# Graph attention layer on one core: preparation and edge stage in one block, no clearing of the sums, first markings inside the q loop, twelve blocks normalised on GpSimd

## The reference

```python
h = relu(layernorm(x))
q, k, v = h @ wq + bq, h @ wk + bk, h @ wv + bv
scores = sum(q[dst] * k[src], -1) / 16 + edge_weight * we + be
attn = softmax of scores over the edges of each dst
out = segment_sum(v[src] * attn, dst)
y = layernorm(h + out + h @ ws + bs) * g1 + b1
z = layernorm(y + gelu(y @ w_ff1 + b_ff1) @ w_ff2 + b_ff2) * g2 + b2
return x + z
```

## Time and profile before

| what | us |
|---|---|
| median of three runs (2398.57 to 2403.62) | 2402.55 |
| profiled execution, its own time | 2402.3 |
| its span, first to last instruction | 2400.5 |
| busy: PE / DVE / ACT / POOL | 2212.3 / 1757.4 / 1168.5 / 1653.7 |
| load of an activation table on ACT | 1.28 |
| a store of 512 KB of h, issue to landing, median | 6.7 |

### The profile page before, as it was taken

The page is one execution under the profiler, slowest core; times in us unless marked ns, Lnnn a source line. Parts: engine busy times, 40 slices in busy tenths (PEclk is TensorE's granted clock), DMA queues, the critical chain, the costliest instruction groups (busy, mean ns, idle before and its releaser), DMA issues. The chain is left out here.

```text
span 2400.5 us, 69609 instructions
## 1 busy us (share of the span) xinstructions
PE 2212.3 (92%) x14709; PEld 1867.1 (78%) x14710; DVE 1757.4 (73%) x7359; ACT 1168.5 (49%) x2903; POOL 1653.7 (69%) x1828
## 2 busy tenths in 40 slices
PE   6789889898999999999999999999999999989995
PEld 4678767776777777877887888888888888877884
DVE  7668667676777777777777777777778888774378
ACT  5545444444444444444444544555445555454454
POOL 4747777777777777777777777777777777402356
PEclk8989999999999999999999999999999999989997
DMA  8344444444444444444444444444444444350014
GB/s 266 103 116 139 137 138 136 137 138 137 139 137 137 136 137 138 138 138 139 136 138 137 137 138 136 138 135 137 137 140 136 139 140 137 89 159 0 0 53 135
DMA packets 148118, 311.09 MB, mean 130 GB/s; under 512 B 33550, under 2 KB 84609, under 8 KB 148088
## 3 DMA queue, kind: packets, MB, share of 16 engines
q0 software_dynamic: 75264, 205.62, 29.7%
q1 hardware_dynamic: 54702, 90.19, 11.7%
q10 hardware_dynamic: 18122, 14.96, 2.0%
HBM read 290.21 MB, written 20.43 MB: 129 GB/s over the span
## 5 line engine op out<-in xcount | busy, mean ns | idle before, releaser
L831 POOL DMA_INDIRECT work<-h_rows,idx x1536 | 1461.4, 951 | 483.2 <-issue 445.4
L919 PE MATMUL bank<-work 128*128 x3520 | 836.5, 380 | 0.0
L1010 DVE SCALAR_TENSOR_TENSOR work<-bank,work 128x257 bf16<-128x257 f32 x1764 | 646.7, 424 | 231.7 <-SPq L795 200.3
L856 PE MATMUL bank<-q,onehot 128*128 x5304 | 740.2, 274 | 70.2 <-DVE work L1010 52.7
L919 PEld LDWEIGHTS bank<-work 128*128 128x128 f32 x3520 | 634.6, 190 | 78.9
L856 PEld LDWEIGHTS bank<-q,onehot 128*128 128x128 bf16 x5304 | 510.2, 98 | 154.6 <-issue 92.6
L967 ACT COPY work<-bank 128x256 f32<-128x256 f32 x880 | 285.5, 377 | 397.5 <-PE bank L906 395.0
L963 ACT ACTIVATE work<-work 128x1 f32<-128x1 f32 x440 | 129.6, 295 | 624.5 <-DVE work L1076 624.5
L1076 DVE CUSTOM_DVE_ANT_0 work<-bank,work 128x512 f32<-128x512 f32 x440 | 329.8, 750 | 108.7 <-PE bank L862 77.1
L964 ACT ACTIVATE work<-work 128x512 f32<-128x512 f32 x440 | 311.6, 708 | 0.0
L906 PE MATMUL bank<-ident,work 128*128 128x128 f32 x1760 | 266.7, 274 | 29.0 <-ACT work L964 29.0
(11 more groups left out here) (192 smaller groups left out, 1601.7 us busy)
## 6 DMA issues: line engine op xcount, KB each, us to landing
dst_words<-dst_short SPq DMA_DIRECT2D x99, 512.0 KB
work<-h_rows,idx POOLq DMA_INDIRECT x1568
bias<-h_rows ACTq DMA_DIRECT2D x56, 128.0 KB
r_rows<-bias ACTq DMA_DIRECT2D x55, 128.0 KB
work<-r_rows SPq DMA_DIRECT2D x49, 128.0 KB, 2.1
acc<-in_x SPq DMA_DIRECT2D x4, 1536.0 KB, 15.7
h_rows<-acc SPq DMA_DIRECT2D x12, 512.0 KB, 6.7
work<-in_x SPq DMA_DIRECT2D x12, 512.0 KB, 3.9
```

The costliest lines, as they stand in the source:

```text
L831: pool.indirect_dma_start(rows[:, u, j, 0:D], None, h_rows, bass.IndirectOffsetOnAxis(idx[:, half, u * J + j:u * J + j + 1], 0)).then_inc( ...
L856: last = nc.tensor.matmul(banks[j][:, 0:D1], onehot[:, k, j, :], q3[:, bass.ds(b, 1), c, 0:D1], start=(c == 0), stop=(c == 2))
L919: last = nc.tensor.matmul(banks[6 + k][:, 0:D1], probs[:, j, :], rows[:, bass.ds(slot, 1), j, :], start=(j == 2), stop=(j == 1))
L1010: last = nc.vector.scalar_tensor_tensor(out=product[:, j, 0:D1], in0=banks[j][:, 0:D1], scalar=SCALE, in1=rows[:, bass.ds(slot, 1), j, :], ...
```

## The change

Preparation and edge stage become one block. The five memsets of `acc` (`clear`) go: a first sum is multiplied by a decay of 0 where a node has edges, and at the end nodes without edges are multiplied by 0 through `inv_sum`. The first two markings, the read of the maxima and what they need stand in DVE's iteration 40 of the q loop (`MARKED_AT`). POOL normalises blocks 28 to 35 and 44 to 47, before its cast of the list and not behind it. `layer_factors` loses a copy. Each engine takes over its part of the edge stage behind its last instruction of the preparation, with waits where the barrier stood. `product` lies before `outside` in SBUF now. The bodies of the edge stage's loops are moved, not changed.

```diff
-    BY_POOL = range(FULL - 8, FULL)
+    BY_POOL = [*range(28, 36), *range(FULL - 4, FULL)]
+    MARKED_AT = 40
...
+        def normalised(b):
+
+            if b in BY_POOL:
+                return h_done_by_pool, BY_POOL.index(b) + 1
+            return h_done, sum(1 for k in range(b + 1) if k not in BY_POOL)
...
-            dve.wait_ge(ln_link, 5 * turn + 5)
-            nc.vector.scalar_tensor_tensor(out=nmr[:, blocks], in0=mean[:, blocks], scalar=-1.0, in1=rstd[:, blocks], op0=ALU.mult, op1=ALU.mult).then_inc(ln_link, 1)
-            dve.wait_ge(ln_link, 5 * turn + 6)
-            nc.vector.tensor_copy(tmp[:, blocks], nmr[:, blocks]).then_inc(ln_done, 1)
+            dve.wait_ge(ln_link, 4 * turn + 5)
+            nc.vector.scalar_tensor_tensor(out=nmr[:, blocks], in0=mean[:, blocks], scalar=-1.0, in1=rstd[:, blocks], op0=ALU.mult, op1=ALU.mult).then_inc(ln_done, 1)
...
             @block.gpsimd
-                pool.wait_ge(list_in, 3 * 16)
-                g.tensor_copy(dst_s[0:EDGE_P, :], dst_a[0:EDGE_P, :]).then_inc(dst_cast, 1)
-
-                pool.wait_ge(ln_done, 4)
-                for n, half in enumerate((BY_POOL[0:4], BY_POOL[4:8])):
+                for n, half in enumerate((BY_POOL[0:4], BY_POOL[4:8], BY_POOL[8:12])):
+                    pool.wait_ge(ln_done, 4 if half[-1] >= QUARTERS[3][0] else 3)
...
+                pool.wait_ge(list_in, 3 * 16)
+                g.tensor_copy(dst_s[0:EDGE_P, :], dst_a[0:EDGE_P, :]).then_inc(dst_cast, 1)
...
-                def clear(k):
-                    first, end = k * XG, (k + 1) * XG if k < 4 else NB
-                    pool.wait_ge(h_out[k], 3 * 16 if k < 4 else 16)
-                    pool.wait_ge(hT_ready, min(end, B))
-                    pool.memset(acc[:, first:end, :], 0.0)
...
-                for k in range(5):
-                    clear(k)
+
+                pool.wait_ge(plan_done, 1)
+                n, m, rounds = counts(pool)
...
             @block.scalar
+                act.wait_ge(plan_done, 1)
+                nc.scalar.activation(decay[:, 1:2], eps[:, 0:1], ACT.Exp, scale=0.0).then_inc(sums_set, 1)
+                act.wait_ge(biases_split, 1)
+                act.wait_ge(h_out[0], 3 * 16)
+                act.dma_start(h_in, h_rows[0:P, :]).then_inc(h_back, 16)
+                act.sem_inc(r_stored, 16)
+                prepare(0, 0)
+                prepare(1, 1)
...
             @block.vector
+                nc.vector.memset(acc[:, 0:FULL, D:D1], 0.0)
...
+                def mark_first_steps():
+
+                    for k in range(4):
+                        dve.wait_ge(h_out[k], 3 * 16)
+                    dve.wait_ge(h_out[4], 16)
+                    dve.wait_ge(tab_copied, 6)
+                    dve.wait_ge(plan_done, 1)
+                    nc.vector.memset(banks[7][:, 0:D1], 0.0).then_inc(sums_set, 1)
+                    dve.load(regs[0:3], steps_tab[0:1, 0:3])
+                    ahead[:] = [dve.snap(v, min_val=0, max_val=TP * BLOCKS) for v in regs[0:3]]
+                    blocks[:] = [block_of(dve, v) for v in ahead]
+                    dve.sem_inc(added, 1)
+                    dve.sem_inc(max_kept, 1)
+                    dve.sem_inc(onehot_done, S)
+                    mark(place_of_mark(ahead[0]), 0)
+                    mark(place_of_mark(ahead[1]), 1)
+                    read_max(0, 0, blocks[0])
...
+                    if b == PLAN + 2:
+                        dve.wait_ge(biases_split, 1)
+                        nc.vector.memset(rows[:, :, :, D:D1], 1.0).then_inc(ones_set, 1)
+                    if b == MARKED_AT:
+                        mark_first_steps()
...
+                dve.wait_ge(lo_done, B)
+                edge_scores(ahead[0], 0, 0, 0)
+                dve.wait_ge(outside_done, 1)
+                mark(place_of_mark(ahead[2]), 0)
+                dve.wait_ge(sums_set, 2)
...
             @block.tensor
+                pe.wait_ge(plan_done, 1)
                 pe.load(regs[0:2], steps_tab[0:1, 0:2])
                 ahead = [block_of(pe, pe.snap(v, min_val=0, max_val=TP * BLOCKS)) for v in regs[0:2]]
                 pe.sem_inc(summed, S)
                 pe.sem_inc(r_copied, 1)
+                pe.wait_ge(identity_added, 1)
+                pe.wait_ge(lo_done, B)
                 pe.wait_ge(onehot_done, S + 1)
                 expand_q(0, 0, ahead[0])
...
-                nc.vector.tensor_tensor(weight_sum, acc[:, :, D], inv_sum, ALU.mult).then_inc(sums_ready, 1)
+                nc.vector.tensor_tensor(weight_sum, acc[:, :, D], inv_sum, ALU.mult)
+                nc.vector.scalar_tensor_tensor(out=inv_sum, in0=acc[:, :, D], scalar=0.0, in1=inv_sum, op0=ALU.is_gt, op1=ALU.mult).then_inc(sums_ready, 1)
```

More of the change, by code:

```diff
@@ L320, in _ @@
                 sp.dma_start(dst_of[:, 0:WC * C], dst_short[0:1, 0:WC * C].to_broadcast((P, WC * C))).then_inc(dst_in, 16)
+                n, m, rounds = counts(sp)
+                regs = [sp.alloc_register(f"free_after{u}") for u in range(G)]
+                sp.sem_inc(slot_free, LEAD)
+                with nc.allow_non_contiguous_dma("columns of biases"):
+                    for t, v, k in ((bff1_col, b_ff1, FC), (g1_col, g1, DC), (b1_col, b1, DC)):
+                        sp.dma_start(t[:], columns(v, k)).then_inc(late_in, 16)
@@ new lines, in _ @@
+                sp.sem_inc(chunk_landed, 1)
+                last = sp.to_reg(rounds * (2 * 16 * NW) + 16)
+                sp.wait_ge(late_in, 7 * 16)
+                sp.wait_ge(dst_in, last)
+                all_turns = sp.alloc_register("all_turns")
+                sp.load(all_turns, n_trips[0:1, 3:4])
+                all_back = sp.to_reg(sp.snap(all_turns, min_val=NW, max_val=B * NW) * 16 + 16)
+                sp.wait_ge(late_in, 7 * 16)
+                sp.wait_ge(h_back, all_back)
+                sp.wait_ge(late_in, 7 * 16)
@@ new lines, in store_r, with trip @@
+                def store_r(turn):
+                    act.wait_ge(r_copied, turn + 2)
+                    act.dma_start(r_rows[bass.ds(turn % B * P, P), :], r_out).then_inc(r_stored, 16)
+                def trip(r, i, steps):
+                    first = act.snap(act.to_reg(r * TP + i * U), min_val=0, max_val=B * TP)
+                    for u in range(steps):
+                        s, k = first + u, u % 2
+                        act.wait_ge(masked_done, s + 1)
+                        nc.scalar.activation(decay[:, k:k + 1], old_max[:, k:k + 1], ACT.Exp, bias=new_max, scale=-1.0)
+                        nc.scalar.activation(probsT, masked, ACT.Exp, bias=new_max, scale=-1.0).then_inc(exp_done, 1)
+                        for half in (1, 0):
+                            act.wait_ge(turned, s * 2 + (2 - half))
+                            nc.scalar.copy(probs[:, 2 * half:2 * half + 2, :].rearrange("p j n -> p (j n)"), banks[5 - half][:, 0:2 * P]).then_inc(probs_done, 1)
+                        prepare(s + 2, k)
+                        for at, body in ((3, copy_hTe), (6, copy_r), (7, store_r)):
+                            if steps == U and u == at:
+                                body(act.snap(act.to_reg(r * NW + i), min_val=0, max_val=B * NW))
@@ L487, in _ @@
+                act.wait_ge(plan_done, 1)
+                trips(act, trip)
             @block.vector
@@ L633, in _, with edge_scores @@
                 third_part(B - 1)
+                def edge_scores(step, r, s, k, meanwhile=None):
+                    chunk = chunk_of(dve, step)
+                    slot = slot_of(dve, chunk)
+                    column = dve.snap(dve.to_reg((chunk - r * TP) * J), min_val=0, max_val=R)
+                    there, first_half, second_half = dve.to_reg(chunk + 1), dve.to_reg(s * 2 + 1), dve.to_reg(s * 2 + 2)
+                    dve.wait_ge(chunk_landed, there)
+                    for half, ready in ((0, first_half), (1, second_half)):
+                        dve.wait_ge(q_edges, ready)
+                        for j in (2 * half, 2 * half + 1):
+                            last = nc.vector.scalar_tensor_tensor(out=product[:, j, 0:D1], in0=banks[j][:, 0:D1], scalar=SCALE, in1=rows[:, bass.ds(slot, 1), j, :],
+                                                                  op0=ALU.mult, op1=ALU.mult, accum_out=dots[:, k, j:j + 1])
+                        last.then_inc(dotted, 1)
+                    if meanwhile:
+                        meanwhile()
+                    dve.wait_ge(dotted, second_half)
+                    nc.vector.tensor_tensor(score[:, k, :], dots[:, k, :], ew_all[:, bass.ds(column, J)], ALU.add).then_inc(scored, 1)
@@ L728, in _ @@
                         nc.tensor.matmul(steps_before, ones[:, 0:1], chunk_left[:, 0:TP + LEAD], start=True, stop=True).then_inc(free_ready, 1)
-        used[0] = EDGE_FIRST
-        masked = part(C)
-        probsT = masked
-        probs = part(C).rearrange("p (j n) -> p j n", j=J)
-        outside = part(C, BF16)[:, 0:2 * C].rearrange("p (k n) -> p k n", k=2)
```

(2 more changed lines are left out.)

438 lines of the change are left out of this document (178 added, 260 removed).

## The result

Device time is 2384.83 us, median of 4 runs (2382.92 to 2386.03), against 2401.61 us of the kernel before on the same chip, median of 4: ratio 0.993, 95% interval 0.9913 to 0.9948. That is 16.8 us less; the forecast was 17.0 less, 2385.3. The profiled execution has a span of 2382.6 (its own time 2384.42) where before's was 2400.5.

What follows compares the result with a forecast made beforehand. POOL's unbroken gathers, or a start paced by them, were taken to bound the edge stage, so its end moves with POOL's restart. Terms 14.5 + 0.5 - 1.0 + 1.8 + 0.8 + 0.4 = 17.0 us off 2402.3 gave 2385.3, range 2380 to 2391.5.

Steps and rivals of the forecast that it cites:

- Clearing, barrier and SP's place (14.5 + 0.5): Seam from q to edge stage: removing memsets and barrier gains 14.5 us, SP's earlier arrival in its loop 0.5.
- dots not released by SP: Sign of a right forecast: step 0's dots no longer end their wait on SP.
- First markings inside the loop (1.0 lost): DVE's iteration 40 of q: 3.7 us of added work costs 1.0 us; bounds nothing to 5.1.
- some 2.9 of a stall are absorbed: q loop: buffers absorb about 2.9 us of a DVE stall, read from its 5.6 us absence in iteration 29.
- POOL takes four more (1.8): Preparation: ACT loses four normalising blocks to POOL, 2.1 us, of which 1.8 us is taken as gain.
- the rival that POOL slows DVE: Preparation: POOL's normalising slows some five DVE instructions by 0.76 us each, 3.8 us in all, giving 2389.1; chance 0.07.
- DVE instructions over 0.5 us between 40 and 47 us: Preparation: sign that the forecast is wrong, DVE instructions lasting that long in that stretch.
- Copies (0.8): Normalisations of the first three quarters: one copy less gains 0.4 us in the first, 0.2 each in the others.
- Last stage (0.4): Last stage: two copies less where DVE sets the pace gain 0.4 us.
- The end follows the restart: Edge stage: its end moves with POOL's restart, since POOL then issues 1535 gather intervals of 1.259 us without a pause.
- rival of the other sign: Edge stage: nothing reaches the end, 2402, chance 0.02; or moved tiles make steps slower, such as 2413, chance 0.02.
- Early gathers: Preparation: POOL's first eight blocks start earlier, so stores and early gathers start some 5 us earlier.

Runs made afterwards that it cites:

- f1_repeat: Changed kernel with the larger of value and 0, instead of a register copy, for each table value a wait is made from; 2380.38 us, ratio 0.9913.
- f5_pool_eight: Against f1_repeat: POOL normalises only the last eight blocks, after its cast, and ACT normalises 28 to 39; 2378.64 us, ratio 0.9912.
- g7: Kernel before, with f1_repeat's register edit and its barrier kept, but POOL doesn't clear the sums; 2387.21 us, ratio 0.9938.
- f6: Against f1_repeat: POOL's clearing of the sums put back behind the early gathers, without a barrier; 2383.23 us, ratio 0.9926.
- e1: Changed kernel with one more register operation (an AND) on each table value a wait is made from; 2553.64 us, ratio 1.0639.
- f2: Against f1_repeat: markings moved to block 44, clearing and load left at 40, DVE's counts loaded before its last preparation wait; 2377.53 us, ratio 0.9905.
- e3: Against e1: bank clearing and register load stay at block 40, the two markings and maximum copy go to block 44; 2556.72 us.
- e2: Against e1: first markings moved out of the q loop, behind the last third part; 2554.41 us.

## Why the prediction was right

*Clearing, barrier and SP's place (14.5 + 0.5).* Measured 30.68 - 15.56 = 15.1, and 15.1 again in f1_repeat; in f5_pool_eight, with the same code in the seam, 16.9, since the clock stayed up behind the first step's wait. Of it 11.4 is the clearing (g7). Taken off in the other order the shares change: the barrier alone, with the clearing left in (f6), gives 9.0, and the clearing then 6.1. One step inside was off both ways: the forecast took the half clock of before's first expansions as given and left a higher one to its bounds. They ran at full speed (1.54, not 2.76), and the clock fell in the first step instead, in PE's wait that ended at 116.94. The label that was to show SP's place (dots not released by SP) was a bad sign: the dots stand 1.11 behind the expansion's start wherever that runs at full speed (after, e1, f1, f2, f6), where before had 2.71 and g7 2.74, and carry SP's name all the same.

*First markings inside the loop (1.0 lost).* Mis-sized: 1.5, from blocks 36 to last (mean 14.2 of six profiles with it in one block, 12.7 of three without). The rule with which it was made, that some 2.9 of a stall are absorbed, is right in kind (e3 and f2: split, 0.3 is left) and too large in size: DVE was away from q for 3.3 (96.23 to 99.50), so 1.8 were absorbed.

*POOL takes four more (1.8).* Mis-sized: about 0.9. The rival that POOL slows DVE was given 0.07 and a price of 3.8; it came about at a tenth of that, and its sign, DVE instructions over 0.5 us between 40 and 47 us, was seen (0.78 and 0.70).

*Copies (0.8).* Block 0 to 20 takes 41.39 and 42.68 in the two kernels of the old order, 41.31 in f5: between 0.1 and 1.4. The first quarter's copy brought 0.2 (ACT starts at 19.74 for 19.95), not 0.4.

*Last stage (0.4).* From the last addition to the end: 301.1 before, 303.1 after, and 300.6 to 303.4 in the others. The gain isn't seen, and one execution's clock there moves more than it.

*What made the sum fit.* The preparation ended 1.72 earlier, near the forecast's 1.6, for another reason than the forecast's. Windows of PE behind the plan's block, the kernel before:

```profile
88.00:92.00 4.00, 4.00 (x14) 0.57 0.39 107
```

and the changed kernel:

```profile
88.00:92.00 4.00, 4.00 (x26) 1.00 0.58 159
```

Both waited about 2 us there, before 1.85, the changed kernel 2.03:

```profile
86.63 0.44 PE L958 MATMUL bank<-ident,acc 128*128 128x128 f32 x2 [2.03 <-ACT work L561]
```

But the clock fell in the first and not in the second. Over the eleven profiles of the table it fell in five (before, e1, e2, f1, g7), and blocks 20 to 36 take 24.2 to 24.3 in these and 22.6 to 22.8 in the others: 1.6, whatever the kernel. Such an outcome, which changes from one execution to another, is called a throw here. The length of PE's wait does not tell which (1.86 in e1, f2 and f5). Of the 1.72, then, some 1.5 is this throw (24.24 less 22.75), luck for the forecast, and the change's own parts in the preparation (0.9, and 0.1 to 1.4 for the copies, less 1.5) come to about nothing. Behind the restart, the 1535 intervals took 1928.2 against 1932.4 (1929 to 1931 in the other kernels on ordinary chips whose loop is not loaded again); so the last gather stands at 2052.82 and not near 2057. The way to the last addition took 1.2 more and the last stage 1.9 more. Together these give the change 4.2 - 1.2 - 1.9 = 1.1 in the two profiles, where the forecast had 0.4. So 17.0 forecast and 16.8 measured agree better than the terms do, and that is luck; the terms' errors, 0.5, 0.9 and 0.4 lost, are within the throw of one execution.

*The end follows the restart.* The argument on which all rested. Six kernels on ordinary chips besides the one before restart between 119.73 and 131.46, and the last addition is restart + 1952.2 to 1955.0 (before 1957.95). No rival of the other sign came about.

*Early gathers.* Forecast 5 us earlier, found at 68.72, 2.2 later than before, and at 65.6 to 67.0 in the second series. The failed step is "the stores, and with them the early gathers, start some 5 us earlier". SP's issues of the stores, before and then after:

```profile
31.73 30.14 SPq L301 DMA_DIRECT2D h_rows<-acc  x13
32.41 29.45 SPq L348 DMA_DIRECT2D h_rows<-acc  x13
```

They end at 61.87 and 61.86. Before, the last store waited for POOL's last blocks (ready at 61.5). After the change all blocks are ready by 55.66, but four stores are still to be issued then, from 55.93 on, 1.4 to 2.0 apart: SP itself sets the pace. The last, issued at 60.82 (61.49 before), landed 6.84 later (3.98 before). It cost nothing, since POOL then waited 14.74 for a slot.

## What to carry to other kernels

When a paced chain of issues (here gathers) has one wait at its head, everything that shortens the way to its first release moves the end one for one, within some 3 us here, and a barrier costs mainly what its last arrival does (11.4 of 15), not what it is (0.5). Work that is put into a loop's queue should be cut into pieces shorter than the buffers' lead: the same markings cost 1.5 in one piece and 0.3 in two. And a short idle time of PE can cost more than its length: behind the same wait of 3.25 the clock fell in one profile and not in another, and the fall cost 2.8. Before such a difference is put down to an edit, look for it between kernels with the same code.

## What the runs showed that was not expected

- With one more register operation on each waited value the loop over steps loaded its code again in every trip: DVE waited 3.3 us instead of 0.5 at the head of each of 55 trips, and the kernel took 169 us more, with its dots and gathers at their usual times.
- A marking (128x512 to bf16, SBUF to SBUF) that began beside a POOL memset lasted until the end of the memset: 8.61 for 0.35, once, in f6.
- PE's clock after a wait of about 2 us differs from one execution to another: 0.57 in some, 1.00 in others, with nearly the same instructions. Behind 3.25 it was the same.
- One chip ran the kernel before in 3279 us instead of 2401, with the same times for gathers and dots, longer waits between engines and a lower mean clock of PE.
